# An index transpose issued directly behind the gathers, and a dot-product reduction ahead of the one-hot compares

## The reference, cut to what matters

```python
_, top_idx = jax.lax.top_k(sim, 8)            # sim = k @ q_i, causal
idx = concatenate([i, top_idx[slots]])        # for each combination of 1 or 2 of the 8 slots
K, V = k[idx], v[idx]
gram = einsum('cnd,cmd->cnm', K, K)
score = log(det(gram) + 1e-06) / size         # softmax over the combinations
out_s = softmax(K @ q_i / 4) @ V              # weighted over the combinations, summed
```

## Time and profile before

| | us |
|---|---|
| median of 3 runs | 6884.42 (6884.02 to 6886.83) |
| the profiled execution | 6877.4 |
| its span | 6875.8 |
| the block with the loop, about | 2794 |
| VectorE busy in it | 2543.78 |
| TensorE busy in it | 2215.66 |
| GpSimd busy in it | 1961.15 |
| ScalarE busy in it | 954.53 |

### The profile page before, as it was taken

One profiled execution on the slowest core, in us unless ns is written; L12 is line 12 of the kernel. 1 busy time (PEld: TensorE's weight loads), 2 busy tenths in 40 slices (PEclk: granted clock), 3 DMA queues, 4 the chain that ended last, 5 costly groups with the idle time before them and its releaser, 6 DMA issues. The chain is left out here.

```text
span 6875.8 us, 140150 instructions
## 1 busy us (share of the span) xinstructions
PE 4948.4 (72%) x45364; PEld 3635.9 (53%) x45365; DVE 4327.4 (63%) x9002; ACT 2060.7 (30%) x6098; POOL 3242.9 (47%) x4341
## 2 busy tenths in 40 slices
PE   5776776987787887788878787334971997169990
PEld 2333333775555555555555555333860776069990
DVE  5777775227998999999999999723654333212223
ACT  3343333223333333333333333222210332123330
POOL 1222222115666676777777677335235000554447
PEclk8677776996766667766676667557985996589995
DMA  4000000002222222222222222212222002111113
GB/s 140 7 5 5 7 3 6 0 4 70 76 73 76 70 76 73 76 73 76 74 75 76 74 73 76 61 35 73 76 72 61 0 0 60 56 48 46 46 42 110
DMA packets 170739, 369.46 MB, mean 54 GB/s; under 512 B 35650, under 2 KB 100939, under 8 KB 169140
## 3 DMA queue, kind: packets, MB, share of 16 engines
q1 hardware_dynamic: 136404, 283.77, 12.6%
q0 software_dynamic: 33792, 78.69, 3.6%
HBM read 286.86 MB, written 75.50 MB: 53 GB/s over the span
## 5 line engine op out<-in xcount | busy, mean ns | idle before, releaser
L2333 POOL TENSOR_TENSOR l2a_prod<-l2a_keys 128x64 f32<-128x64 f32 (+1 forms) x2304 | 1141.2, 528 | 614.8 <-ACT l2a_norms L2224 610.7
L2678 PE MATMUL l2a_g<-l2a_feat,l2a_onehot 128*128 128x33 bf16 x27648 | 831.9, 188 | 26.4 <-issue 19.0
L2678 PEld LDWEIGHTS l2a_g<-l2a_feat,l2a_onehot 128*128 128x128 bf16 x27648 | 811.3, 104 | 30.7 <-issue 23.3
L2544 DVE TENSOR_SCALAR l2a_onehot<-l2a_spread,l2a_key_col 128x2048 bf16<-128x2048 bf16 x576 | 560.2, 999 | 177.5 <-DMA l2a_spread<-index_rows 140.9
L2647 PE MATMUL l2a_s<-l2a_qkT 32*128 32x128 f32 (+1 forms) x1536 | 618.9, 494 | 52.5 <-issue 52.4
L1734 POOL TENSOR_TENSOR l_hc<-l_hs,l_bc 128x512 f32<-128x512 f32 x192 | 243.1, 1266 | 797.8 <-DVE l_hs L1808 793.1
L1903 PE MATMUL l_y<-l_hc,l_selT 128*96 128x512 f32 x384 | 312.2, 908 | 294.2 <-POOL l_hc L1734 294.2
L2553 DVE TENSOR_REDUCE l2a_dots<-l2a_prod 128x72 f32<-128x1152 f32 x384 | 514.9, 1341 | 2.6 <-POOL l2a_prod L2339 2.6
L2222 ACT COPY l2a_keys<-l2a_g 128x128 f32<-128x128 f32 x768 | 200.5, 261 | 836.4 <-PE l2a_g L2678 825.0
L440 POOL DMA_INDIRECT rows_in<-l3f_dispatch_xn,l3f_dispatch_at x128 | 123.0, 961 | 652.1 <-ACT l3f_dispatch_xn L416 613.4
L2659 PE MATMUL l2a_t<-l2a_ident_bf,l2a_index 128*16 128x128 bf16 x384 | 94.9, 247 | 446.2 <-ACT l2a_index L2205 446.1
(11 more groups left out here) (403 smaller groups left out, 11368.7 us busy)
## 6 DMA issues: line engine op xcount, KB each, us to landing
l2a_spread<-index_rows SPq DMA_DIRECT2D x384, 512.0 KB, 3.7
rows_in<-main_zeros SPq DMA_DIRECT2D x1, 13824.0 KB, 59.8
l2f_xg<-rows_in SPq DMA_DIRECT2D x72, 192.0 KB, 2.4
rows_out<-l2f_ys POOLq DMA_DIRECT2D x72, 192.0 KB, 2.4
l3f_xg<-rows_in SPq DMA_DIRECT2D x72, 192.0 KB, 2.4
rows_out<-l3f_ys POOLq DMA_DIRECT2D x72, 192.0 KB, 2.4
l3f_w<-in_l3f_w SPq DMA_DIRECT2D x2, 4608.0 KB, 33.3
l_xT<-in_l_xT SPq DMA_DIRECT2D x16, 384.0 KB, 3.8
```

The lines of the kernel that those rows point to most:

```text
L2333: nc.gpsimd.tensor_tensor(made[:, j, at:at + wide * wide, :].rearrange("p (b a) f -> p b a f", b=wide), key[:, lo:lo + wide, :].unsqueeze( ...
L2544: ins = nc.vector.tensor_scalar(onehot[:, s[2] % 2, kt, :, :].rearrange("p k t -> p (k t)"), spread[:, s[2] % 2, :, :].rearrange("p k t -> ...
L2678: ins = nc.tensor.matmul(g_ps[j][:, a * FEAT:(a + 1) * FEAT], onehot[:, s[2] % 2, kt, j * SLOTS + a, :], feat3[:, s[1], kt, piece, h, :], ...
```

## The change

On ScalarE `copy_turned` moves from the end of the body to directly behind `cast_index`, so ahead of all stages and of `front`. On TensorE `turn_index` moves from the end of the body to directly behind the two gathers, so ahead of `turn_output` and `front`. On VectorE the reduction to `dots` moves ahead of the compares. No instruction is added, removed or resized, and no wait is changed except in its place.

```diff
 ScalarE body
                     if real:
                         cast_index(n, u, i)
+                        copy_turned(n, u, i)
...
                     if i == 0 and real:
                         split_middle(n, u)
-                    if real:
-                        copy_turned(n, u, i)
 VectorE body
+                    s = back(5)
+                    if s:
+                        q, t = count_of(s), s[2] // PAIRS
+                        dve.wait_ge(S["prod_ready"], counted(q + 1))
+                        h = t * HEADS + first_head(s[2])
+                        nc.vector.tensor_reduce(dots[:, h:h + 4:3, :], prod[:, s[2] % 3, :, :, :], AX.X, ALU.add
+                                                ).then_inc(S["dots_ready"], 1)
                     s = back(2)
                     if s:
...
                         ins.then_inc(S["onehot_ready"], 1)
-                    s = back(5)
-                    if s:
...
 TensorE body
                     if s3:
                         gather(s3, 0)
                         gather(s3, 1)
+                    if not (isinstance(n, int) and n == B):
+                        turn_index(n, u, i)
                     if previous(n, u, i, OUT):
                         turn_output(*previous(n, u, i, OUT))
                     nxt = next_image(n, u, last)
                     if nxt and FRONT <= i < FRONT + 8:
                         front(*nxt, i - FRONT)
-                    if not (isinstance(n, int) and n == B):
-                        turn_index(n, u, i)
```

## The result

Four runs of the changed kernel have a median of 6997.69 us (6988.74 to 7011.31), four of the kernel before 6885.62. The ratio is 1.0164 with a 95% interval of 1.0143 to 1.0184: 112 us slower, where 77 us faster was forecast. It lies outside the range of 6715 to 6905, on the side of the rival in which TensorE becomes the bound.

The account below looks back on a forecast made before the run. VectorE was taken to bound the kernel, 91% busy, waiting for the index chain. Savings of 4.5 us per even and 0.3 per odd image, 16 x 4.8 = 77 us, gave 6800 profiled, 6807 us median; range 6715 to 6905.

Parts of the forecast that it names:

- TensorE becomes the bound: Rival: from body 8 to the next image's score TensorE is late; 42 us slower, 6926 us; chance 0.17.
- What bounds it: In the block VectorE sets the pace, 91% busy; 177.5 us idle ahead of the compares, mostly the late index chain.
- The copy: ScalarE's copy follows its turn by about 0.5 us, row out 6 us earlier; its wait, 192 us in all, is free.
- The reduction under `weigh`: In body 8 the reduction ahead of the compares runs during GpSimd's `weigh`, saving VectorE 1.27 us per image.
- TensorE's price: Each part of `front` stands behind the turn, so the round trip through ScalarE is bare: 5.6 us per image.
- So TensorE just keeps up even at the lower clock.: Bodies 3 to 7: TensorE needs 8.9 us per body, VectorE takes 8.7.
- d: Delay of turn 11, built up on TensorE from body 8 on: 2.1 us, bounds 0.5 and 6.
- pair: One even and one odd image: 4.8 us saved, 16 times per run; each us of d beyond 2.1 costs one in both.
- Both signs: Signs that TensorE bounds: VectorE waiting for scores in many bodies, or a clock under 0.6.
- TensorE doesn't hold it: Rival: clock stays high through the parts of `front`, d about nothing; 182 us faster, 6702 us; chance 0.17.
- The turn is not what is late: Rival: the DMAs alone pace the short bodies, only the reduction counts; 20 us faster, 6864 us; chance 0.16.
- The sentence on the clock gate: Skill passage cited for the slower rival: waits between bursts send TensorE's array back to half its clock each time.

Follow-up runs that it names:

- the filler: Six unused 128-column matmuls per body ahead of TensorE's wait for the cast, added to the kernel without TensorE's move: 6836.26 us, 0.9912 of before.
- after: The changed kernel with all three edits, against the kernel before: median 6997.69 us, ratio 1.0164; its profiled execution took 7011.31 us.
- filler in all bodies: Six unused matmuls ahead of the cast wait in all twelve bodies: changed kernel 6829.71 us, kernel without TensorE's move 6836.26, kernel before 6886.81.

## Why the prediction was wrong, by its steps

**What bounds it.** Right: VectorE, with its idle time ahead of the compares, late for the index chain. Removing that wait without TensorE's move did make the kernel faster, by 0.5%, and by 0.9% with the filler.

**The copy.** Right: copies start 0.3 to 0.5 us behind their turns in all bodies of after (medians by the timeline), ScalarE's wait cost nothing that shows in the run with the copy alone, and the idle time ahead of the compares is 61.0 us where about 60 was forecast.

**The reduction under `weigh`.** Right where it was looked for: the two compares of body 8 take 1.85 us in even images and 2.2 in odd ones (medians; 1.8 forecast, 3.10 in the earlier trace rows). Wrong as a sum: with VectorE's edit alone the compares' mean rose to 1057 ns, and the time did not fall. I counted the collision with GpSimd that goes, and none that comes. The filled wait puts VectorE's work on top of GpSimd's products in other places.

The Trainium skill (SBUF — State Buffer, "Who interferes with whom") bears on this with a second rule that I did not weigh: a VectorE instruction with two inputs in SBUF contends with a GpSimd instruction that reads SBUF. In the kernel without TensorE's move the gap stage's product, which has two such inputs, went from 368 to 565 ns beside products of GpSimd that went from 528 to 553, while the reduction, which the page excepts, took 1333 ns against 1341. That agrees in kind; no run here takes GpSimd's products away, so the cause of the growth is argued and not shown.

**TensorE's price: the step that failed.** "So TensorE just keeps up even at the lower clock." Two things were wrong in what was built on it. The numbers of this part are means over images 5 to 29, counted from 0, of the two traces.

The first is TensorE's lateness. Its rate was right (8.8 us per body from turn 4 to turn 8, 8.9 forecast), and VectorE's is even a little slower: 9.2 us per body from `found` to `found` in after and 9.1 before (8.7 forecast, taken between compares). But TensorE comes to body 4 late, its turn 5.4 us behind the end of `found`, and so small a margin makes up only 1.5 us of it by body 8. In the kernel before it is 3.3 us late in body 4 and 0.3 in body 8, because its parts of `front` run where it would otherwise wait. The prediction left turn 8 where it was; it comes 3.9 us behind `found`.

The second is the clock. From body 8 on the pieces were taken from times of the kernel before, part 6 between the two levels, as if its clock stayed. It didn't: the move bares the 0.69 us in every body from 3 to 10, and in that order TensorE was granted 0.50 in the first image and 0.57 over the block, against 0.88 and 0.68. From turn 8 to turn 11 it is 28.5 us, 27.1 forecast, 24.6 before.

So d, forecast at 2.1 us, is (28.5 - 24.6) + (3.9 - 0.3) = 7.5 us, past the 4.5 from which the slower rival decides and past the upper bound of 6. The sum of that rival with this d gives 4.8 - 2 x 5.4 = -6.0 us per pair, 96 us slower. The first image adds 19 us, which a sum over a settled pair can't see: 115 us, where 112 lie between the medians and 134 between the profiled executions. Measured, a pair is 7.5 us slower; whether the 1.5 left over are VectorE's longer instructions (81.5 us per image, 80.3 before) no run shows.

With the clock raised by filler in all bodies, the same order has d = 0.3 us (25.3 us from the end of `found` of body 8 to turn 11, 24.9 before). So the round trip in its new place, priced at 5.6 us per image, costs nothing that shows, and what the changed kernel loses comes with the lower clock.

**The rivals.** "TensorE becomes the bound" was the right one, with the right place, and was given 0.17. Both signs that the prediction named for it came: VectorE waits for scores 41 times (50.7 us), and the clock is under 0.6 (0.57). What spoke against it, that TensorE's 18 us of idle time per image "would have to be lost nearly all", was no argument: in after TensorE still idles for (2910 - 2513.9) / 32 = 12 us per image, since an engine is late in one stretch and idle in another. "TensorE doesn't hold it" (6702) falls also for the two kernels with filler in all bodies that were faster, which come to 6830 and 6836. "The turn is not what is late" falls with the wait ahead of the compares, 61.0 us: with the reduction alone moved it is 135.1.

The sentence on the clock gate (the Trainium skill, TensorE: Matmul & The Clock Gate, "HAM oscillation — how this bites in real kernels") was the best warning at hand, and I let it bear on d by one part only. The Trainium skill has a second case beside it (TensorE: Matmul & The Clock Gate, "A second HAM failure mode: psum-queue depth-cycling") that fits closer: short idle times between groups of matmuls, often enough, make the clock go to and fro. The trace agrees in that short idle times are enough: with 0.69 us idle in each 9.31 us TensorE had the lower level through the whole stretch from 1610 to 1650 us, at 93% busy, and with them filled it had 1.00. In that stretch the clock did not go to and fro; it stayed low.

## What to carry to other kernels

Independent work on TensorE that stands between its output and its next input from another engine is cover for the round trip, and moving it behind the wait can cost the engine's clock besides the time: look at the granted clock of the stretch before and after, and if a wait must stand bare and TensorE is the bound, try a few matmuls without use in it. To price a moved item, carry the engine's lateness from body to body instead of comparing rates, and don't count idle time in one stretch as reserve for another. Of idle time removed on VectorE beside a busy GpSimd, expect part to come back as longer instructions: here 80 of 120 us in one kernel, and all of 42 in another.

## What the runs showed of the hardware that was not expected

- With one idle time of 0.69 us in each body of 9.31 us TensorE stayed at the lower of its two levels: 0.50 at 37.06 of 40 us busy. With six short matmuls in it (0.50 us at the higher level) the same stretch has 1.00 at 38.07 of 40. Six such matmuls a few hundred ns later, behind the turn, change nothing in the clock (0.50), and cost 145 us over the changed kernel.
- Leaving out half of the projections lowered the clock of the kernel before in the block, from 0.68 to 0.60, and its time hardly moved (0.9980): less work on TensorE took as long as before (2215.34 us busy, 2215.66 before), at a lower clock.
- The mean of VectorE's two-input products in the gap stage went from 368 to 565 ns by the order of instructions around them alone.
